# A two-layer recurrent kernel: waits for low halves moved into the last pass of each product, the choice of experts split and moved, its counting matmuls in bf16

## The chip, the cores and the metric

The kernel runs on one core of a Trainium2 chip. The metric is the device time of one execution in microseconds; the median of several executions is compared. The engines are TensorE (PE; its weight loads are shown as PEld), VectorE (DVE), ScalarE (ACT), GpSimd (POOL) and SyncE (SP, which here only issues DMAs).

## What is computed

The input is x of shape (8, 512, 128) in float32. Two layers follow, each of the form x = x + s * silu(f), where s is a sequence mixer and f a feed-forward branch, both of the layer-normed x.

```python
# second layer, attention branch: a memory MLP per head (w0, w1), 8 heads, chunks of 64 tokens
ss = rmsnorm(seq, store_norm_g)
kv = ss @ w_kv                            # keys, values per head
grads = grad(chunk_loss)(mem_ws, keys, lr, values)
momentum = assoc_scan(mom_gate, -grads)   # over the chunks
updates = assoc_scan(1 - decay, momentum)
x = q @ (mem_w0 + updates[0])
vals = silu(x) @ (mem_w1 + updates[1])
out = (rmsnorm(vals) * (mh_gamma + 1) * gate) @ w_combine
# second layer, feed-forward branch: one of 8 experts for each token
aff = x @ centroids.T
eid = argmax(aff, axis=-1)
alpha = sigmoid(sum(x * centroids[eid]))
out = x + alpha * (relu(ln(x)[expert eid] @ w1[eid] + b1[eid]) @ w2[eid] + b2[eid])
```

The first layer (a gated linear recurrence and a binarized MLP) is not touched by the change.

## The kernel before

The attention branch is computed without ever forming the updated memories: the update of a chunk is a sum over earlier tokens, so that each application of an updated memory is a plain product plus a causal sum of scores times gradients. The scores have 4 row tiles of 128 tokens; the coefficients of the two scans (`m.coef`) are multiplied onto them.

**The heads.** `heads` runs 65 steps over 64 pairs (batch, head). In one step three pairs are in work, and each engine's code for it is one function `step(f, s, z)`: `f` is the pair whose first half is done (keys, the gradient, the first application, which ends as `xs`), `s` the pair before it, in its second half (scores of `xs` against `s_sb`, second application, `vals`, the product with `w_combine`), `z` the pair before that, whose head output is normalized and added to `acc`. Each engine has its own queue and goes through `step` in the order in which it is written; between engines there are only semaphores (`p_`, `a_`, `v_`, `g_` for those that PE, ACT, DVE and POOL raise).

**High and low halves.** Products that need more precision than one pass gives are split: the high half is a rounded copy (fp32r), the low half the difference. `product` then makes three passes into one bank, high times high, high times low and low times high. The high halves are cast on ACT (`s_high` L1053, `qa_high` L1066, `xs_high` L1047, `err_high` L1073). The low halves are subtracted on DVE (`xs_low` in `low_rows`, L1266; `err_low`, L1335) and on POOL (`s_low` and `qa_low` in `lacks`, L1455). PE waits for the low half before the first of the three passes:

```python
for j, (u, v) in enumerate(((0, 0), (0, 1), (1, 0))):
    last = pe.matmul(out, left[u], right[v], start=start and j == 0, stop=stop and j == 2)
```

**A step on PE** goes: projections U, EB and QA (`project`), the scores of `s` (`scores`, three passes for row tiles 0 and 1, then plain float32 matmuls, L790), the product of `w1` with `s_sb` into EB, the same with `xs` into VB and the causal sum (`apply`, L798), four transposes of `err` (L939), the product of `w4t` with `err` into U, the scores of `f`, four transposes of `du`, the projection with `w_x`, `apply`, and at the end the rows out (L978) and sums of squares (L982). In five of the eight batches a block of 128 tokens of the experts runs between these.

**Extras of the first steps.** The last batch's preparation is finished within the heads: in step 0 (`n == 0`) `last_weights`, the normalized last rows (two on ACT, two on POOL in `last_rows_normalized`, L1461) and their transposes (`last_turned`, L832); in step 1 `last_products`. The experts are chosen on DVE in `choose` (9 operations, L1170 to L1178), called in step 1 (`k == 0`) after `weigh` of `s`. The tokens of each expert are then counted on PE in `routing`, two float32 matmuls with 256 columns in steps 2 and 3.

**The tail.** In the last steps DVE also adds up finished batches (`last_sum` L1389, `add_rows` L1396), and in the last step (`final(s)`) it makes `xs_low`, the means, the weighing, `acc`, one `add_rows` for batch 6, `attention_before_last_head` (L1404, L1405), the last means (L1261) and `finish`.

## Time and profile before

| | |
|---|---|
| Median of 3 runs | 1088.19 us (1088.04 to 1088.26) |
| The profiled execution, own time | 1087.95 us |
| Its span | 1086.2 us |
| PE busy | 1058.4 us, 97% of the span |
| DVE busy | 688.6 us, 63% |
| ACT busy | 674.7 us, 62% |
| POOL busy | 558.9 us, 51% |
| Share of the chain that ended last: PE, POOL, DVE | 90%, 4%, 2% |

The granted clock of TensorE was 0.997 of full speed over the span. A busy PE says only that matmuls were in flight, since they are pipelined; whether PE waited is seen in the distance between the starts of two matmuls.

### The profile page before, as it was taken

The page shows a single profiled execution, that of the slowest core. Times are in us where ns is not written, and L with a number is a line of the kernel's source. Part 1 is how long each engine was busy: PE and PEld are TensorE (multiplying, and loading weights), DVE is VectorE, ACT ScalarE, POOL GpSimd, SP SyncE. Part 2 cuts the span into 40 slices and gives each one's busy share as a digit, 9 for nine tenths or more (in the row PEclk, how much of TensorE's full clock was granted, in tenths as well). Part 3 has the DMA queues.
Part 4 walks back from the last instruction along what each step waited for, and adds up shares of the span by engine and source line. Part 5 has one row for each costly group of instructions (what it writes and reads, how often), then busy time and mean ns, then how long its engine had stood idle before and what let it go on. Part 6 is the DMA issues. An engine that isn't in the chain of part 4 may idle for free.

```text
span 1086.2 us, 19002 instructions
## 1 busy us (share of the span) xinstructions
PE 1058.4 (97%) x6595; PEld 892.7 (82%) x6595; DVE 688.6 (63%) x1757; ACT 674.7 (62%) x1353; POOL 558.9 (51%) x571
## 2 busy tenths in 40 slices
PE   6899899999999999999999999999999999999996
PEld 5566788888888888888888888888888888888885
DVE  5787777777755565556555555655565555556786
ACT  6777566676665565656555655656565556566774
POOL 5885444588874344434444443444344444444553
PEclk9999999999999999999999999999999999999998
DMA  7210300000220000000000000000000000004220
GB/s 210 75 53 20 117 1 1 3 31 20 67 59 4 16 11 11 8 19 10 11 8 9 20 11 6 11 21 8 9 10 12 18 9 6 6 3 118 71 70 26
DMA packets 41953, 32.53 MB, mean 30 GB/s; under 512 B 4010, under 2 KB 36492, under 8 KB 41724
## 3 DMA queue, kind: packets, MB, share of 16 engines
q1 hardware_dynamic: 38262, 25.83, 8.3%
q0 software_dynamic: 2272, 4.67, 1.4%
q8 instruction: 54, 0.88, 0.3%
q10 hardware_dynamic: 1326, 0.82, 0.3%
q14 instruction: 39, 0.32, 0.1%
HBM read 18.23 MB, written 13.34 MB: 29 GB/s over the span
## 4 chain that ended last, share of the span: by engine, by line
PE 90%; POOL 4%; DVE 2%; issue 1%; ACT 1%; DMA 0%; ACTq 0%; POOLq 0%; DVEq 0%
PE bank L775 40%; PE bank L798 22%; PE bank L790 6%; PE bank L978 5%; PE bank L933 3%; PE bank L970 3%; PE bank L958 3%; PE bank L939 2%; PE bank L982 2%; PE bank L326 1%; POOL xn L248 1%; POOL rr L264 1%; PE bank L378 1%; PE bank L349 1%; POOL r L244 0%
## 5 line engine op out<-in xcount | busy, mean ns | idle before, releaser
L1222 DVE TENSOR_TENSOR p_sb<-bank,coef 128x512 f32<-128x512 f32 (+3 forms) x512 | 218.4, 482 | 5.0 <-PE bank L775 4.9
L1497 POOL TENSOR_TENSOR sq_rest<-sq,sq_high 128x450 f32<-128x450 f32 x63 | 66.1, 1049 | 238.4 <-ACT sq_high L1097 238.4
L798 PE MATMUL bank<-p_sb,err_t 128*128 128x450 f32 x504 | 130.8, 402 | 0.0
L798 PE MATMUL bank<-p_sb,du_t 128*128 128x450 f32 (+3 forms) x512 | 128.9, 395 | 0.1
L798 PEld LDWEIGHTS bank<-p_sb,err_t 128*128 128x128 f32 x504 | 82.5, 190 | 44.1 <-DVE p_sb L1222 23.7
L1501 POOL TENSOR_TENSOR sq_low<-sq_rest,sq_mid 128x450 bf16<-128x450 f32 x63 | 66.4, 1054 | 97.7 <-ACT sq_mid L1111 97.3
L798 PEld LDWEIGHTS bank<-p_sb,du_t 128*128 128x128 f32 x512 | 82.1, 190 | 41.7 <-issue 23.3
L1279 DVE SCALAR_TENSOR_TENSOR acc<-bank,rg,acc 128x128 f32<-128x128 f32 x220 | 61.7, 343 | 65.4 <-POOL rg L1479 65.4
L1344 DVE SCALAR_TENSOR_TENSOR du<-q_sb,bank 128x512 f32<-128x512 f32 x64 | 44.0, 688 | 83.2 <-PE bank L775 83.1
L1472 POOL TENSOR_TENSOR rs<-ms,neg_half 128x4 f32<-128x4 f32 (+1 forms) x65 | 80.7, 1242 | 30.6 <-DVE ms L1253 24.7
L1051 ACT ACTIVATE s_sb<-bank 128x512 f32<-128x512 f32 x64 | 38.3, 598 | 87.7 <-PE bank L775 87.7
L1455 POOL TENSOR_TENSOR s_low<-s_sb,s_high 128x512 fp32r<-128x512 f32 x64 | 82.6, 1291 | 15.9 <-ACT s_high L1053 15.8
L1045 ACT ACTIVATE xs<-bank 128x450 f32<-128x450 f32 x64 | 35.0, 547 | 89.3 <-PE bank L798 89.3
L1093 ACT COPY vals<-bank 128x450 f32<-128x450 f32 x63 | 33.7, 535 | 81.1 <-PE bank L798 81.1
L1354 DVE TENSOR_TENSOR xl_all<-bank,xl_all 128x128 f32<-128x128 f32 x39 | 11.4, 292 | 114.3 <-PE bank L970 114.3
L1511 POOL DMA_INDIRECT ffn_rows<-xl_all,ids x39 | 40.4, 1037 | 81.9 <-DVE xl_all L1354 81.9
L1455 POOL TENSOR_TENSOR qa_low<-qa,qa_high 128x450 fp32r<-128x450 f32 x64 | 74.2, 1159 | 14.1 <-ACT qa_high L1066 12.7
L1071 ACT COPY err<-bank 128x512 f32<-128x512 f32 x64 | 37.6, 587 | 60.2 <-PE bank L775 59.5
L978 PE MATMUL bank<-w_out,vals 128*128 128x128 f32 x504 | 66.2, 274 | 0.0
L1108 ACT COPY du_t<-bank 128x512 f32<-128x512 f32 x64 | 37.6, 587 | 35.6 <-PE bank L958 35.6
L978 PEld LDWEIGHTS bank<-w_out,vals 128*128 128x128 f32 x504 | 59.1, 179 | 0.0
L790 PE MATMUL bank<-qa,yb 128*128 128x66 f32 (+1 forms) x256 | 52.8, 288 | 0.0
(341 smaller groups left out, 3089.7 us busy)
## 6 DMA issues: line engine op xcount, KB each, us to landing
sorted_rows<-coef SPq DMA_DIRECT2D x5, 516.0 KB, 5.2
rows<-sorted_rows SPq DMA_DIRECT2D x39, 64.5 KB, 1.8
ew<-in_L_ffn_w SPq DMA_DIRECT2D x8, 256.0 KB, 4.1
x<-in_L_attn_inputs SPq DMA_DIRECT2D x7, 256.0 KB, 5.6
x_rows<-x SPq DMA_DIRECT2D x7, 256.0 KB, 2.3
attn_out<-acc SPq DMA_DIRECT2D x7, 256.0 KB, 2.1
ew<-attn_out SPq DMA_DIRECT2D x7, 256.0 KB
ew<-ffn_rows SPq DMA_DIRECT2D x8, 192.0 KB
```

Source lines behind the costliest of these rows:

```text
L775: last = pe.matmul(out, left[u], right[v], start=start and j == 0, stop=stop and j == 2)
L790: last = pe.matmul(out, left[:, (i - 2) * P:(i - 1) * P], right[:, P * i:], start=True, stop=True)
L798: last = pe.matmul(out[:, P * i:QW], rows[:, i, :], p_sb[:, P_COL[i]:P_COL[i] + QW - P * i], start=False, stop=True, skip_group_check=True)
L978: pe.matmul(VB[0:r, t * P:t * P + P], vals[:, t * P:t * P + r], m.w_out[:, s[1], :], start=True, stop=True)
L1222: last = nc.vector.tensor_tensor(dst, src, w, ALU.mult)
L1279: last = nc.vector.scalar_tensor_tensor(sums, o, g, sums, ALU.mult, ALU.add)
L1344: nc.vector.scalar_tensor_tensor(du[:], q_sb[:], 0.5, U[:], ALU.mult, ALU.mult).then_inc(v_du, 1)
L1455: nc.gpsimd.tensor_tensor(parts[1][:], whole[:], parts[0][:], ALU.subtract).then_inc(done, 1)
L1472: nc.gpsimd.tensor_tensor(rs[:, part], ms[:, part], m.neg_half[:, 0:T][:, part], ALU.pow).then_inc(g_rs, 1)
L1497: nc.gpsimd.tensor_tensor(sq_rest[:], sq[:], sq_3[0][:], ALU.subtract).then_inc(g_rest, 1)
L1501: nc.gpsimd.tensor_tensor(sq_3[2][:], sq_rest[:], sq_3[1][:], ALU.subtract).then_inc(g_lo, 1)
L1511: nc.gpsimd.indirect_dma_start(m.ffn_rows, bass.IndirectOffsetOnAxis(ids[r][:, 0:1], axis=0), y[r], None).then_inc(s_y[r], 16)
```

## The change

It has these parts.

1. `product` makes its passes in the order high-high, low-high, high-low (left, right), so that the right side's low half is used in the last pass only. With `low=` PE waits for that half just before the last pass, and for the high half before the first. This is used at four places of a step: scores of `s` (`v_xl`), the product with `s_sb` (`g_sl`), with `err` (`v_el`), scores of `f` (`g_ql`).
2. `choose` is cut in two. `ranked` (the four operations that find the best expert) runs in step 1 after `err_low`, and the rest after `weigh` of `f` at the end of DVE's step 1.
3. The one-hot choice and the two constant matrices of the counting matmuls are made in bf16: two casts on DVE in `choose`, and `routing` takes them. They lie in the second half of `oh`'s old space.
4. Two of the last four rows are normalized on DVE in place of POOL, ahead of `q_sb` in step 0. `last_turned` stands on PE ahead of the transposes of `err`.
5. In the last step `add_rows` for batch 6 runs on DVE before `weigh`.

```diff
-            def product(out, left, right, start=True, stop=True):
-                for j, (u, v) in enumerate(((0, 0), (0, 1), (1, 0))):
+            def product(out, left, right, start=True, stop=True, low=None):
+
+                for j, (u, v) in enumerate(((0, 0), (1, 0), (0, 1))):
+                    if j == 2 and low is not None:
+                        pe.wait_ge(*low)
                     last = pe.matmul(out, left[u], right[v], start=start and j == 0, stop=stop and j == 2)
...
-                        last = product(out, [part[:, i * P:i * P + P] for part in left_2], [part[:, P * i:] for part in right_2])
+                        last = product(out, [part[:, i * P:i * P + P] for part in left_2], [part[:, P * i:] for part in right_2], low=low if i == 0 else None)
...
-                    pe.matmul(FREE, m.upper[:], flat, start=True, stop=True).then_inc(p_routed, 1)
+                    pe.matmul(FREE, upper16, flat, start=True, stop=True).then_inc(p_routed, 1)
                 if c == 2:
-                    pe.matmul(FREE, m.ones[:], flat, start=True, stop=True).then_inc(p_routed, 1)
+                    pe.matmul(FREE, ones16, flat, start=True, stop=True).then_inc(p_routed, 1)
...
-                    pe.wait_ge(v_xl, k + 1)
+                    pe.wait_ge(a_xh, k + 1)
                     pe.wait_ge(v_p0, SC_BANKS * (k + 1))
-                    scores(s_2[s[1] % 2], xs_2, s_sb[s[1] % 2][:, 2 * P:], xs, p_s1)
+                    scores(s_2[s[1] % 2], xs_2, s_sb[s[1] % 2][:, 2 * P:], xs, p_s1, low=(v_xl, k + 1))
...
-                    pe.wait_ge(g_sl, n + 1)
+                    pe.wait_ge(a_sh, n + 1)
...
-                    product(EB[:], [w[:] for w in w1], [part[:] for part in s_2[h % 2]], start=False).then_inc(p_e, 1)
+                    product(EB[:], [w[:] for w in w1], [part[:] for part in s_2[h % 2]], start=False, low=(g_sl, n + 1)).then_inc(p_e, 1)
...
                 if f is not None:
+                    if n == 0:
+                        last_turned()
                     pe.wait_ge(a_err, n + 1)
...
-                    if n == 0:
-                        last_turned()
-                    pe.wait_ge(v_el, n + 1)
+                    pe.wait_ge(a_eh, n + 1)
                     pe.wait_ge(v_q, n + 1)
-                    product(U[:], [w[:, 3, :] for w in m.w4t], [part[:] for part in err_2]).then_inc(p_d, 1)
+                    product(U[:], [w[:, 3, :] for w in m.w4t], [part[:] for part in err_2], low=(v_el, n + 1)).then_inc(p_d, 1)
...
-                    pe.wait_ge(g_ql, n + 1)
+                    pe.wait_ge(a_qh, n + 1)
...
-                    scores(yk, qa_2, yw, qa, p_s0, SC_ORDER[:-1])
+                    scores(yk, qa_2, yw, qa, p_s0, SC_ORDER[:-1], low=(g_ql, n + 1))
...
+            def last_rows_normalized():
+                for k in range(2, T):
+                    row = NT - T + k
+                    last = nc.vector.tensor_scalar(m.xl_all[:, row, 0:D], m.x_last[:, k, :], m.mv[:, row, 0:1], m.rr[:, 1, row:row + 1], ALU.subtract, ALU.mult)
+                last.then_inc(v_last, 1)
...
-            def choose():
+            def ranked():
 
                 link(nc.vector.tensor_reduce(top, m.aff, AX.X, ALU.max))
                 link(nc.vector.tensor_tensor(oh, m.aff, bc(top), ALU.is_equal))
                 link(nc.vector.tensor_tensor(oh, oh, m.rank_f[:], ALU.mult))
                 link(nc.vector.tensor_reduce(best, oh, AX.X, ALU.max))
-                nc.vector.tensor_tensor(oh, m.rank_f[:], bc(best), ALU.is_equal).then_inc(v_oh, 1)
+
+            def choose():
+
+                nc.vector.tensor_copy(upper16, m.upper[:])
+                nc.vector.tensor_copy(ones16, m.ones[:])
+                nc.vector.tensor_tensor(oh16, m.rank_f[:], bc(best), ALU.is_equal).then_inc(v_oh, 1)
...
                 if final(s):
                     low_rows(k)
                     means(l)
+                    add_rows(B - 2)
                     dve.wait_ge(p_x, k + 1)
...
-                    if k == 0:
-                        dve.wait_ge(g_last, POOL_LAST["roots"])
-                        dve.wait_ge(a_last, ACT_LAST["products"])
-                        choose()
                 if f is not None:
+                    if n == 0:
+                        last_rows_normalized()
                     dve.wait_ge(a_th, n + 1)
...
+                    if n == 1:
+                        dve.wait_ge(a_last, ACT_LAST["products"])
+                        ranked()
                 for c in summed(z)[1]:
-                    if c < B - 1:
+                    if c < B - 2:
                         add_rows(c)
...
                     weigh(f, p_s0, v_p0, n, s)
+                    if n == 1:
+                        dve.wait_ge(g_last, POOL_LAST["roots"])
+                        choose()
...
-                    if n == 0:
-                        last_rows_normalized()
                     scatter(s, 0)
```

DVE in step 1, before, from the last piece of `weigh` of `s` (`p_sb`) on; the tiles named `ew` are scratch of the choice:

```order
L1222 TENSOR_TENSOR p_sb<-bank,coef 128x256
L1170 TENSOR_REDUCE ew<-amd 128x32
L1171 TENSOR_TENSOR ew<-amd,ew 128x256
L1172 TENSOR_TENSOR ew<-ew,rank_f 128x256
L1173 TENSOR_REDUCE ew<-ew 128x32
L1174 TENSOR_TENSOR ew<-rank_f,ew 128x256
L1175 RECIPROCAL ew<-rr 128x32
L1176 TENSOR_TENSOR rr<-rr,ew 128x32
L1177 TENSOR_TENSOR ew<-ew,rr 128x32
L1178 TENSOR_TENSOR ew<-ew 128x32
L1328 SCALAR_TENSOR_TENSOR q_sb<-bank,s_sb 128x512
```

The same place now, to the end of `choose` (in between, `weigh` of `f` with the taking of the gates, L1256):

```order
L1240 TENSOR_TENSOR p_sb<-bank,coef 128x256
L1345 SCALAR_TENSOR_TENSOR q_sb<-bank,s_sb 128x512
L1347 SCALAR_TENSOR_TENSOR q_sb<-thu,q_sb 128x512
L1352 TENSOR_TENSOR err_low<-err,err_high 128x512
L1183 TENSOR_REDUCE ew<-amd 128x32
L1184 TENSOR_TENSOR ew<-amd,ew 128x256
L1185 TENSOR_TENSOR ew<-ew,rank_f 128x256
L1186 TENSOR_REDUCE ew<-ew 128x32
L1364 SCALAR_TENSOR_TENSOR du<-q_sb,bank 128x512
```

```order
L1240 TENSOR_TENSOR p_sb<-bank,coef 128x256
L1190 CAST ew<-upper 128x128
L1191 CAST ew<-ones 128x128
L1192 TENSOR_TENSOR ew<-rank_f,ew 128x256
L1193 RECIPROCAL ew<-rr 128x32
L1194 TENSOR_TENSOR rr<-rr,ew 128x32
L1195 TENSOR_TENSOR ew<-ew,rr 128x32
L1196 TENSOR_TENSOR ew<-ew 128x32
L1170 TENSOR_SCALAR lr_gate<-lr_gate 128x8x8
```

Nine operations no longer stand between `weigh` and `q_sb`; four stand behind `err_low`, and seven, two of them new, behind the last `p_sb` and ahead of the rates (`lr_gate`) and the gates.

PE in a step without extras, before, from the scores of `s` to the product with `s_sb`:

```order
L775 MATMUL bank<-xs_high,s_high 128x450 [waits v_p0,v_xl]
L775 MATMUL bank<-xs_low,s_high 128x450
L775 MATMUL bank<-xs_high,s_low 128x450
L775 MATMUL bank<-xs_high,s_high 128x322
L775 MATMUL bank<-xs_low,s_high 128x322
L775 MATMUL bank<-xs_high,s_low 128x322
L790 MATMUL bank<-xs,s_sb 128x66
L790 MATMUL bank<-xs,s_sb 128x194
L775 MATMUL bank<-s_high,w1n_high 128x512 [waits g_sl]
L775 MATMUL bank<-s_low,w1n_high 128x512
L775 MATMUL bank<-s_high,w1n_low 128x512
```

And now:

```order
L782 MATMUL bank<-xs_high,s_high 128x450 [waits v_p0,a_xh]
L782 MATMUL bank<-xs_high,s_low 128x450
L782 MATMUL bank<-xs_low,s_high 128x450 [waits v_xl]
L782 MATMUL bank<-xs_high,s_high 128x322
L782 MATMUL bank<-xs_high,s_low 128x322
L782 MATMUL bank<-xs_low,s_high 128x322
L797 MATMUL bank<-xs,s_sb 128x66
L797 MATMUL bank<-xs,s_sb 128x194
L782 MATMUL bank<-s_high,w1n_high 128x512 [waits a_sh]
L782 MATMUL bank<-s_high,w1n_low 128x512
L782 MATMUL bank<-s_low,w1n_high 128x512 [waits g_sl]
```

The number of matmuls is the same; the pass with the right low half (`xs_low`, `s_low`) is the third, and the wait for it stands there.

DVE at the start of step 0, before and now (`xl_all<-x_last` are the two rows):

```order
L1429 SCALAR_TENSOR_TENSOR nm_last<-mv,rr 128x4
L1328 SCALAR_TENSOR_TENSOR q_sb<-bank,s_sb 128x512
L1330 SCALAR_TENSOR_TENSOR q_sb<-thu,q_sb 128x512
L1142 TENSOR_TENSOR w_x_low<-bank,w_x_high 128x512
L1151 TENSOR_SCALAR ew<-ew 128x384 x2
```

```order
L1452 SCALAR_TENSOR_TENSOR nm_last<-mv,rr 128x4
L1154 TENSOR_SCALAR xl_all<-x_last,mv,rr 128x128 x2
L1345 SCALAR_TENSOR_TENSOR q_sb<-bank,s_sb 128x512
L1347 SCALAR_TENSOR_TENSOR q_sb<-thu,q_sb 128x512
L1149 TENSOR_TENSOR w_x_low<-bank,w_x_high 128x512
```

The two rows stand ahead of `q_sb` and so of all that DVE does in step 0.

## Rows read from the trace of the kernel before

**Rows 1.** Groups by form, 300 to 1000 us: count | busy us, mean ns | idle before.

```profile
L775 PE MATMUL bank<-y_high,w_v_high 128*128 128x512 f32 x45 | 17.8, 395 | 0.0
L775 PE MATMUL bank<-y_high,w_v_low 128*128 128x512 f32 x45 | 17.7, 394 | 0.0
```

**Rows 2.** Timeline of step 1: start, us, instruction, idle before and its releaser.

```profile
127.41 0.41 DVE L1170 TENSOR_REDUCE ew<-amd 128x32 f32<-128x256 f32 x1
...
128.50 0.62 ACT L1073 CAST err_high<-err 128x512 fp32r<-128x512 f32 x1
...
129.23 0.42 DVE L1174 TENSOR_TENSOR ew<-rank_f,ew 128x256 f32<-128x256 f32 x1
...
130.26 0.60 PE L939 MATMUL bank<-ident,err 128*128 128x128 f32 x4
...
130.51 0.68 DVE L1328 SCALAR_TENSOR_TENSOR q_sb<-bank,s_sb 128x512 f32<-128x512 f32 x1
...
131.83 0.68 DVE L1335 TENSOR_TENSOR err_low<-err,err_high 128x512 fp32r<-128x512 f32 x1
...
132.57 0.50 PE L775 MATMUL bank<-err_high,w4t_high 128*128 128x512 f32 x1 [1.72 <-DVE err_low L1335]
```

**Rows 3.** Timeline, the end of step 1 and the start of step 2.

```profile
137.21 1.04 POOL L1501 TENSOR_TENSOR sq_low<-sq_rest,sq_mid 128x450 bf16<-128x450 f32 x1 [3.79 <-ACT sq_mid L1111]
137.30 1.85 DVE L1151 TENSOR_SCALAR ew<-ew 128x128 f32<-128x128 f32 x2
...
140.12 0.16 DVE L1252 TENSOR_SCALAR ms<-bank 128x3 f32<-128x3 f32 x1 [0.78 <-DVE ew L1153]
...
141.96 0.37 PE L775 MATMUL bank<-xs_high,s_high 128*128 128x450 f32 x1
```

**Rows 4.** Timeline of step 0.

```profile
110.89 1.28 POOL L1455 TENSOR_TENSOR s_low<-s_sb,s_high 128x512 fp32r<-128x512 f32 x1
...
111.40 0.69 DVE L1328 SCALAR_TENSOR_TENSOR q_sb<-bank,s_sb 128x512 f32<-128x512 f32 x1 [0.40 <-ACT thu L1055]
...
114.96 0.69 DVE L1335 TENSOR_TENSOR err_low<-err,err_high 128x512 fp32r<-128x512 f32 x1 [0.19 <-ACT err_high L1073]
...
115.48 1.18 POOL L1455 TENSOR_TENSOR qa_low<-qa,qa_high 128x450 fp32r<-128x450 f32 x1 [0.86 <-ACT qa_high L1075]
...
116.78 0.69 DVE L1344 SCALAR_TENSOR_TENSOR du<-q_sb,bank 128x512 f32<-128x512 f32 x1 [0.17 <-PE bank L775]
```

**Rows 5.** Timeline, a counting matmul (step 2) and the scores behind it.

```profile
147.93 0.59 PE L812 MATMUL bank<-ew,upper 128*128 128x256 f32 x2
...
148.56 0.37 PE L775 MATMUL bank<-qa_low,y_high 128*128 128x450 f32 x1
```

**Rows 6.** Timeline, scores and the product with s_sb, steps 62 and 63.

```profile
1046.61 0.71 PE L790 MATMUL bank<-xs,s_sb 128*128 128x66 f32 x4
1047.33 0.50 PE L775 MATMUL bank<-s_high,w1n_high 128*128 128x512 f32 x1
...
1060.57 0.71 PE L790 MATMUL bank<-xs,s_sb 128*128 128x66 f32 x4
1061.06 0.50 PE L775 MATMUL bank<-s_high,w1n_high 128*128 128x512 f32 x1
```

**Rows 7.** Timeline of the tail.

```profile
1071.29 0.63 DVE L1266 TENSOR_TENSOR xs_low<-xs,xs_high 128x450 fp32r<-128x450 f32 x1 [1.38 <-ACT xs_high L1047]
...
1071.97 0.47 PE L775 MATMUL bank<-xs_high,s_high 128*128 128x450 f32 x1 [0.71 <-DVE xs_low L1266]
...
1072.97 1.69 DVE L1222 TENSOR_TENSOR p_sb<-bank,coef 128x512 f32<-128x512 f32 x4 [0.92 <-PE bank L775]
...
1075.60 0.68 DVE L1396 TENSOR_TENSOR ew<-ew 128x512 f32<-128x512 f32 x1
...
1076.91 0.69 DVE L1405 TENSOR_TENSOR ew<-ew 128x512 f32<-128x512 f32 x1
...
1077.64 0.59 DVE L1261 TENSOR_SCALAR ms<-bank 128x1 f32<-128x1 f32 x4
```

More of the change, by code:

```diff
@@ L694, in attend @@
         oh = early(NT, E)
+        half = oh.rearrange("p n e -> p (n e)").bitcast(BF16)
+        oh16 = half[:, 0:NT * E].rearrange("p (n e) -> p n e", e=E)
+        upper16, ones16 = half[:, NT * E:NT * E + P], half[:, NT * E + P:NT * E + 2 * P]
         cnt, run = early(E, NT), early(E, NT)
@@ L728, in attend @@
         ACT_LAST = {"w_x": 1, "xl": 2, "w_qk": 3, "y": 4, "products": 5, "sums": 6}
-        DVE_LAST = {"nm": 1, "w_x": 2, "w_qk": 3, "y": 4, "gates": 5}
-        POOL_LAST = {"xl": 1, "roots": 2}
+        DVE_LAST = {"nm": 1, "xl": 2, "w_x": 3, "w_qk": 4, "y": 5, "gates": 6}
+        POOL_LAST = {"roots": 1}
         LAST_W = {"w_x": (m.w_x, m.qt, m.mem0, 5), "w_qk": (m.w_qk, m.qt, m.kt, 6)}
@@ L781, in project, with scores @@
                 return product(out[:, 0:width], [part[:, at[1], :] for part in w], y, stop=stop)
-            def scores(left_2, right_2, left, right, done, tiles=SC_ORDER):
+            def scores(left_2, right_2, left, right, done, tiles=SC_ORDER, low=None):
                 for i in tiles:
@@ L804, in routing @@
                 c = first_head(s)
-                flat = oh.rearrange("p n e -> p (n e)")
+                flat = oh16.rearrange("p n e -> p (n e)")
                 if c == 0:
@@ L829, in last_turned @@
                 pe.wait_ge(a_last, ACT_LAST["xl"])
-                pe.wait_ge(g_last, POOL_LAST["xl"])
+                pe.wait_ge(v_last, DVE_LAST["xl"])
                 for k in range(T):
@@ L1197, in places @@
                 link(nc.vector.tensor_tensor(m.aff, m.aff, run.rearrange("p e n -> p n e"), ALU.add))
-                link(nc.vector.tensor_tensor(m.aff, m.aff, oh, ALU.mult))
+                link(nc.vector.tensor_tensor(m.aff, m.aff, oh16, ALU.mult))
                 link(nc.vector.tensor_reduce(pos, m.aff, AX.X, ALU.add))
@@ L1455, in lacks @@
                 nc.gpsimd.tensor_tensor(parts[1][:], whole[:], parts[0][:], ALU.subtract).then_inc(done, 1)
-            def last_rows_normalized():
-                pool.wait_ge(m.g_r1, B)
-                for k in range(2, T):
-                    n = NT - T + k
-                    last = nc.gpsimd.tensor_scalar(m.xl_all[:, n, 0:D], m.x_last[:, k, :], m.mv[:, n, 0:1], m.rr[:, 1, n:n + 1], ALU.subtract, ALU.mult)
-                last.then_inc(g_last, 1)
             def step(f, s, z):
```

## The prediction

> **What bounds the kernel now.** The table shows TensorE busy for 97% of the span and on 90% of the chain that ended last. A busy PE may still wait, so I went through the starts of its matmuls step by step, taking the same matmul in every step as the yardstick. In the middle of the kernel there is nothing to gain: the steps are alike (13.74 us without experts: L790 from 1046.61 to 1060.57, less a wait of 0.22 in between, [rows 6]), and a matmul with a semaphore wait before it is no longer than one without: `y_high,w_v_high`, which waits for `a_dt`, takes 395 ns, `y_high,w_v_low`, which waits for nothing, 394 [rows 1]. The time that a schedule can change lies at the ends. In step 1 PE stands 1.72 us for `err_low`, because DVE, in order, first worked through the choice of experts [rows 2]. In steps 6, 7, 8, 61 and 62 PE starts a product late because its low half is. In the last step it stands 0.71 us for `xs_low`, and then DVE is the last: the last means wait for DVE, not for PE [rows 7].
>
> **The terms.** The sum is made against the profiled execution (1087.95 us, span 1086.2), 0.24 us under the median of the three runs.
>
> *Step 1, the choice.* DVE begins the choice at 127.41 and reaches `q_sb` at 130.51; `err_low` starts at 131.83 and PE's product at 132.57 [rows 2]. Without the choice there, `q_sb` starts 3.10 us earlier, at 127.41, and `err_low` could at 128.73, but `err_high` is there only at 129.12. So `err_low` runs from 129.15 to 129.85, ahead of the end of PE's transposes (130.86) [rows 2]. The wait is gone altogether. PE's next matmul overlaps a long one before it by 0.22 (1060.57 + 0.71 against 1061.06) [rows 6], so 1.72 + 0.22 = 1.94 us. The four operations of `ranked` (127.41 to 129.23, 1.8 us) now follow `err_low`, on this clock from 129.5 to 131.3; `du` behind them needs the three passes of some 0.4 us that start at 130.6, so not before 131.6: hidden, with 0.3 us to spare.
>
> *The rest of the choice.* It now stands behind the last `p_sb` of step 1: one comparison and four small operations, 1.3 us from L1174's start to `q_sb` [rows 2], and two new casts of 128 columns, at 0.1 to 0.2 each (as the second of L1151's pieces below: 0.13 once free), so 1.6 us if nothing holds it. But POOL's `sq_low` runs there: L1151, at 137.30, two pieces of 128 columns, took 1.85 us. The first can be read off the merged row: `sq_low` ends at 138.25 and only then does a piece of this size get through [rows 3]. A cast or a comparison of two SBUF tensors at this place, between 137.1 and 138.25, waits in the same way, and POOL's next operation (`starts`) may hold the small multiplications once more to about 139.0. So I put the end of `choose` at 139.8 (1.6 if free: 138.7). L1151 then comes when POOL is idle and takes 0.5 in place of 1.85, so DVE reaches the means at about 140.6 in place of 140.12 [rows 3]. ACT waits for `v_top` before it takes `xs`: that sets back `xs_high`, `xs_low` and `s_high` by some 1.1 us against PE's order. `xs_low` would end at 142.6 on this clock, while the third pass of the scores, where it is now waited for, is due at 141.96 + 0.41 = 142.37: PE stands about 0.28. `s_low`, behind `s_high` on POOL, costs as much again. I take a loss of 0.55 us; the bounds are 0 (nothing held) and 1.2 (casts and comparison each held by a POOL operation of its own).
>
> *Counting in bf16.* The two float32 passes of L812 take from 147.93 to where the scores begin to flow. `qa_low` starts at 148.56, normally 0.2 behind `qa_high`, so L812 costs 0.43 us of PE [rows 5]. In bf16 one pass of 256 columns remains: a quarter of the time if the passes go by columns, 0.11, and up to 0.19 if something of the next pass's weight load can't hide under so short a one. Saved 0.24 to 0.32 each, twice: 0.5.
>
> *Low halves in the last pass.* In step 62 the product with `s_sb` starts 0.72 behind L790, in the undisturbed step 63 it starts 0.49 behind: 0.22 us lost to `s_low` [rows 6]. Five such places read 0.12, 0.17, 0.22, 0.29 and 0.21 us by the same yardstick, together 1.0. The third pass starts 0.5 us or more behind the first, longer than any of these waits, so all are gained. In the other 58 steps the low half is there in time and nothing changes; the cover is that PE is late anyway, and without it the price of a late half is now reduced by 0.4 to 0.5.
>
> *Step 0.* Here two terms meet. `last_turned` fills time in which PE waits for `err`, and the product with `err` may start at `err_high`, so its third pass is due at once with `err_low`, some 0.5 us earlier than now; but `du` waits for `w_qk_low` on DVE, so at most 0.26 of it reaches the weighing. Against it stand the two rows on DVE, ahead of `q_sb`. On their own they cost 0.3 each. But POOL's `s_low` runs from 110.89 to 112.17 just then [rows 4]. If they are held as L1151 was [rows 3], `q_sb` starts not at 111.40 but near 112.45. POOL no longer slows the gate terms afterwards, which gives about 0.6 back, and `err_low` would start at 115.2 to 115.45 instead of 114.96. `qa_low` on POOL starts at 115.48 [rows 4], a hair later. If `err_low` is first, step 0 gains about 0.1; if it is behind, it waits until 116.66 and the step loses 0.9. I take 0.1, bounds -0.9 and 0.26.
>
> **A rule of the Trainium skill.** The profile shows a DVE operation released at the end of a POOL operation [rows 3]. The page "SBUF — State Buffer" (section "SBUF: two separate sides") says why: VectorE and GpSimd share one port pair under an exclusive lock, taken by whichever starts first for its whole instruction, and a VectorE operation needs it with two SBUF inputs or in a two-port mode. The trace agrees with it in L1151. It speaks against this change at three places: the rows, the casts, the comparison; with it at its full price the result is the first rival's time, without it the sum would be 0.55 better.
>
> *The tail.* `xs_high` is ready at 1071.26, `xs_low` (0.63 long) ends at 1071.92, and PE starts its first pass at 1071.97 [rows 7]. Now two passes run before that and the third starts at 1071.97: it started 0.52 later before. So PE is 0.52 us earlier from there. On DVE the weighing could start at 1072.45, but `add_rows` (0.60 from start to start) now stands before it, from 1071.98 to 1072.58, so it starts 0.39 earlier than 1072.97. What followed `acc` loses the same `add_rows` of 0.60: L1405, before at 1076.91, and the means at 1077.64 come 0.39 + 0.60 = 0.99 earlier, at 1076.65. PE's sums, which the means also need, were there at about 1077.17 by the starts of their matmuls in the timeline, so now at 1076.65: they just meet. Behind this POOL and DVE go on alone, unchanged. 0.98 us, bounds 0.5 (only PE's share) and 1.0.
>
> **Sum.** 1.94 - 0.55 + 0.5 + 1.0 + 0.1 + 0.98 = 3.97 us. 1087.95 - 3.97 = 1083.98; with the 0.24 to the median, 1084.2.
>
> **The rivals.**
>
> *POOL holds DVE at each place.* `err_low` falls behind `qa_low` in step 0 (-0.9 in place of +0.1) and the choice costs 1.2 in place of 0.55. For it: the 0.03 to 0.3 us of margin at 115.48 [rows 4], and that L1151 was held in full. Against it: `err_low` is still computed to be first, and POOL has less to do. 3.97 - 1.0 - 0.65 = 2.3: 1085.9 us. Chance 0.2.
>
> *The low halves buy nothing.* If what delays PE in the five places and the tail follows it (POOL's chain begins with PE's own results, so an earlier PE could meet the next late half), 1.0 and up to 0.5 are missing: 2.5 us, 1085.7. Against it: each chain has slack of over 0.3 in the next product. Chance 0.1.
>
> *A wait inside a product costs PE.* Four waits stand between passes in each of some 63 steps, 252 in all. A wait before a first pass costs nothing that 395 against 394 ns could show [rows 1], but no row has one inside an accumulation. At 16 ns each the whole gain is gone; from 25 ns the kernel is slower by more than 0.2%; at 35 ns it is 8.8 - 4.0 = 4.8 us slower: 1093 us. The mechanism would be a weight load that can't be brought forward past the wait. Against it: the product's first pass has the same load behind a wait and shows none. Chance 0.05.
>
> *Nothing is held.* The two rows and the choice slip past POOL: 3.97 + 0.55 + 0.15 = 4.7: 1083.5. Chance 0.15.
>
> **Chances and range.** The forecast itself, between 1083.8 and 1085.0, has 0.5. With the free case below and the held one above, 1083.2 to 1086.2 holds 8 in 10. The measurement tells about 0.2% (2.2 us) from no change, so faster means under 1086.0: 0.86; within it 0.1; slower 0.04.
>
> **What would show it.** PE's product with `err` in step 1 starts within 0.4 us of the transposes. The counting matmuls are single bf16 rows, and steps 2 and 3 are 0.25 shorter. The scores in step 2 stand for `xs_low` by 0.3, or not at all. In steps 61 and 62 the distance of 0.72 is 0.49. The last means start 1 us earlier, counted from `xs_low`. In step 0 the start of `err_low` against that of `qa_low` decides 1 us. The prediction is wrong if the passes of the middle steps grow longer, or if a DVE operation ahead of `du` is held beyond 131.6.

## The result and the profile after

The changed kernel takes 1082.07 us in the median of 4 runs (1081.69 to 1082.58), the kernel before 1088.22 (1088.04 to 1089.08, 4 runs). The ratio is 0.9939, with a 95% interval of 0.9927 to 0.9951: 6.1 us faster, where 4.0 were forecast, and below the stated range. Its profiled execution is the slowest of the four, 1082.58 us with a span of 1080.8; against that of before it is 5.37 us faster.

A step of PE is measured here from the first matmul `y_high,w_u_high` of a step to that of the next, in the timelines of both profiled executions. Grouped, they say where the time came from:

| PE's steps | before, us | after, us | gain | forecast |
|---|---|---|---|---|
| ahead of step 0 (first layer) | 108.59 | 108.85 | -0.26 | 0 |
| 0 | 12.86 | 13.00 | -0.14 | 0.1 |
| 1 | 18.44 | 16.51 | 1.93 | 1.94 |
| 2 and 3 | 28.30 | 27.92 | 0.38 | -0.05 |
| 6, 7, 8, 61, 62 | 70.19 | 68.75 | 1.44 | 1.0 |
| 4, 5, 9 to 16, 56 to 60 | 205.87 | 204.94 | 0.93 | 0 |
| 17 to 55 (with experts, mostly) | 613.17 | 612.85 | 0.32 | 0 |
| 63 and the tail | 28.79 | 28.01 | 0.78 | 0.98 |

The part ahead of step 0, which the change does not touch, differs by up to 1.5 us between the executions profiled for this study (107.93 to 109.39); that is more than the spread between the four executions of either kernel (1.0 and 0.9 us). The lengths of the steps without experts from 4 on repeat within 0.03 us where an edit does not touch them. Some steps with experts do not repeat as well: step 50 differs by up to 0.35 us between kernels that are the same there, and it is 0.31 longer in the trace after than in that before.

The DVE timeline of the kernel after, at the places of [rows 2, 3, 4, 7] (start, duration, engine, line, operation; in brackets the idle time before it and its releaser):

```profile
111.17 1.60 DVE L1154 TENSOR_SCALAR xl_all<-x_last,mv,rr 128x128 f32<-128x128 f32 x2
112.69 0.68 DVE L1345 SCALAR_TENSOR_TENSOR q_sb<-bank,s_sb 128x512 f32<-128x512 f32 x1
...
115.82 0.69 DVE L1352 TENSOR_TENSOR err_low<-err,err_high 128x512 fp32r<-128x512 f32 x1
...
127.84 0.68 DVE L1345 SCALAR_TENSOR_TENSOR q_sb<-bank,s_sb 128x512 f32<-128x512 f32 x1
...
129.58 0.69 DVE L1352 TENSOR_TENSOR err_low<-err,err_high 128x512 fp32r<-128x512 f32 x1 [0.33 <-ACT err_high L1080]
...
131.55 0.42 DVE L1186 TENSOR_REDUCE ew<-ew 128x32 f32<-128x256 f32 x1
132.13 0.69 DVE L1364 SCALAR_TENSOR_TENSOR du<-q_sb,bank 128x512 f32<-128x512 f32 x1 [0.16 <-PE bank L782]
...
135.56 0.22 DVE L1190 CAST ew<-upper 128x128 bf16<-128x128 f32 x1
135.69 0.22 DVE L1191 CAST ew<-ones 128x128 bf16<-128x128 f32 x1
135.83 1.26 DVE L1192 TENSOR_TENSOR ew<-rank_f,ew 128x256 bf16<-128x256 f32 x1
137.02 0.34 DVE L1193 RECIPROCAL ew<-rr 128x32 f32<-128x32 f32 x1
...
140.18 0.63 DVE L1284 TENSOR_TENSOR xs_low<-xs,xs_high 128x450 fp32r<-128x450 f32 x1 [0.78 <-ACT xs_high L1054]
...
1066.63 0.63 DVE L1284 TENSOR_TENSOR xs_low<-xs,xs_high 128x450 fp32r<-128x450 f32 x1 [1.39 <-ACT xs_high L1054]
...
1067.91 1.67 DVE L1240 TENSOR_TENSOR p_sb<-bank,coef 128x512 f32<-128x512 f32 x4
...
1072.26 0.22 DVE L1279 TENSOR_SCALAR ms<-bank 128x1 f32<-128x1 f32 x2
1072.95 0.22 DVE L1279 TENSOR_SCALAR ms<-bank 128x1 f32<-128x1 f32 x2 [0.46 <-PE bank L881]
```

The same execution on POOL, at the two places where DVE is held:

```profile
111.15 1.28 POOL L1478 TENSOR_TENSOR s_low<-s_sb,s_high 128x512 fp32r<-128x512 f32 x1
115.73 1.78 POOL L1478 TENSOR_TENSOR qa_low<-qa,qa_high 128x450 fp32r<-128x450 f32 x1 [3.30 <-ACT qa_high L1082]
...
135.69 1.12 POOL L1515 TENSOR_TENSOR sq_low<-sq_rest,sq_mid 128x450 bf16<-128x450 f32 x1 [1.92 <-ACT sq_mid L1118]
```

And PE: step 0's wait, and in step 1 the product of [rows 2], which stood 1.72 us and now follows its transposes at once:

```profile
115.57 0.40 PE L782 MATMUL bank<-err_high,w4t_low 128*128 128x512 f32 x1
116.56 0.50 PE L782 MATMUL bank<-err_low,w4t_high 128*128 128x512 f32 x1 [0.59 <-DVE err_low L1352]
...
130.69 0.60 PE L948 MATMUL bank<-ident,err 128*128 128x128 f32 x4
131.05 0.48 PE L782 MATMUL bank<-err_high,w4t_high 128*128 128x512 f32 x1
```

So the two rows hold `q_sb` in step 0 until 112.69, and the comparison is held by `sq_low` (1.26 us, starting 0.14 behind it), both as computed. The counting matmul is one bf16 row, and the second pass of the scores starts 0.34 behind it, where in [rows 5] it was 0.63:

```profile
146.66 0.28 PE L819 MATMUL bank<-ew 128*128 128x256 bf16 x1
...
147.00 0.37 PE L782 MATMUL bank<-qa_high,y_low 128*128 128x450 f32 x1
```

What was not computed is the middle of the kernel. It is visible in a row that the prediction did not use: the weight loads (PEld) of the product with `s_sb`, grouped by line and form. The last columns are busy time, mean ns and the idle time before them with its releaser; first the kernel before:

```profile
L775 PEld LDWEIGHTS bank<-s_high,w1n_high 128*128 128x128 f32 x64 | 12.1, 189 | 3.8 <-POOL s_low L1455 1.2
```

and after:

```profile
L782 PEld LDWEIGHTS bank<-s_high,w1n_high 128*128 128x128 f32 x64 | 12.2, 190 | 0.9
```

2.9 us of idle time at this one load are gone. Step by step in the trace before, 1.31 of the 3.8 lie in the five steps that I had counted, and another 1.31 in the fifteen other steps without experts, 4, 5, 9 to 16 and 56 to 60; after the change both are 0.

### The profile page after: what moved, and what is told of

Read it like the earlier page. It is cut to its first block, busy times and chain, and to the rows that moved or that the text cites. A ratio compares the mean times of both kernels' runs of the same rounds, so it can differ in the third digit from the quotient of the medians.

```text
span 1080.8 us, 18999 instructions
## 1 busy us (share of the span) xinstructions
PE 1055.8 (98%) x6593; PEld 892.0 (83%) x6593; DVE 689.8 (64%) x1761; ACT 674.6 (62%) x1353; POOL 557.4 (52%) x569
## 4 chain that ended last, share of the span: by engine, by line
PE 92%; POOL 4%; DVE 1%; issue 1%; ACT 1%; DMA 0%; ACTq 0%; POOLq 0%; DVEq 0%
PE bank L782 40%; PE bank L805 22%; PE bank L797 6%; PE bank L985 5%; PE bank L977 3%; PE bank L940 3%; PE bank L965 3%; PE bank L948 3%; PE bank L989 2%; PE bank L326 1%; POOL xn L248 1%; PE bank L349 1%; POOL rr L264 1%; PE bank L378 1%; PE bank L282 1%
```

## The experiments

Twelve kernels ran. The edits are against the changed kernel where the label begins with a or n, against the kernel before where it begins with b. Step lengths are PE's, as above.

### The order of the passes alone (b0_order_only)

```diff
-                for j, (u, v) in enumerate(((0, 0), (0, 1), (1, 0))):
+                for j, (u, v) in enumerate(((0, 0), (1, 0), (0, 1))):
```

> The kernel before with the passes of a product in the new order alone; every wait stays before the first pass. Theory (what was missed is a wait of some 0.06 us for the low half of s_sb in every step without experts): the order alone gives nothing, 1088.2 us, and steps 9 to 16 stay at 13.73 us. Rival (the order of the passes shortens the passes themselves): those steps fall to 13.67 and the time to about 1086.7 us.

Measured: 1087.26 us (11 runs) against 1088.05, ratio 0.9993 (0.9984 to 1.0002). No step but one with experts (27, by 0.16) moved by more than 0.05 us, and the steps 9 to 16 did not become shorter (13.74), which refutes the rival. So the order by itself shows no gain clear of noise. The median is 0.8 us lower all the same, within its interval; the profiled executions differ by 0.1.

### Part 1 alone (b1_low_only)

```diff
+                    if j == 2 and low is not None:
+                        pe.wait_ge(*low)
...
-                    pe.wait_ge(g_sl, n + 1)
+                    pe.wait_ge(a_sh, n + 1)
...
-                    product(EB[:], [w[:] for w in w1], [part[:] for part in s_2[h % 2]], start=False).then_inc(p_e, 1)
+                    product(EB[:], [w[:] for w in w1], [part[:] for part in s_2[h % 2]], start=False, low=(g_sl, n + 1)).then_inc(p_e, 1)
```

(and the same for the three other products, with the new order)

> The kernel before with part 1 alone, new order and waits for the low halves before the third pass. Theory: 1.4 us from 24 steps without experts, 1.0 from the five places, 0.5 in the tail, and in steps 0 and 1 another 0.3 and 0.55 because two passes now run during the waits there: 3.7 us faster, 1084.5 us. Rival (low halves are worth only what was forecast): 2.3 us, 1085.9 us, with steps 9 to 16 at 13.73 us.

Measured: 1083.77 us (5 runs), ratio 0.9956 (0.9942 to 0.9969). 4.3 of the 6.1 us are part 1. By steps: 0.26 in step 0, 0.43 in step 1, 0.12 in steps 2 and 3, 1.42 in the five steps, 0.88 in the fifteen other steps without experts, 0.48 in the tail. Another 0.58 in the steps 17 to 55 is there with the new order alone too (612.59 here, 612.58 in b0), and 0.80 was lost ahead of step 0.

### All waits before the first pass, high and low (a1_wait_first)

```diff
-                    if j == 2 and low is not None:
+                    if j == 0 and low is not None:
```

> The changed kernel with all four waits for low halves back before the first pass. Theory: steps 9 to 16 at 13.72 us again, the five places and the tail lose 1.5, step 2 another 0.5 or more since xs_low and s_low are late there: 3.4 us slower than the changed kernel, about 1085.5 us. Rival (the gain beyond the forecast is elsewhere): 1.5 to 2 us slower, about 1084 us.

Measured: 1088.39 us (11 runs), ratio 1.0001 (0.9992 to 1.001): nothing is left of the gain, where I had expected about half. The steps 9 to 16 take 13.79 us, more than before the change (13.73). Here the first weight load of the product with `s_sb` waits for two semaphores. It starts 114 or 115 ns after `s_low` ends, and the matmul behind it 144 to 146 ns, in each of the twenty steps without experts from 4 to 62. With one wait (before, and in the next two kernels) these are 51 to 53 ns for the load and 53 or 54 ns for the matmul. Step 12 of this kernel (`s_low` ends at about 281.90):

```profile
280.61 1.29 POOL L1478 TENSOR_TENSOR s_low<-s_sb,s_high 128x512 fp32r<-128x512 f32 x1
```

```profile
282.01 0.19 PEld L782 LDWEIGHTS bank<-s_high,w1n_high 128*128 128x128 f32 x1
...
282.04 0.47 PE L782 MATMUL bank<-s_high,w1n_high 128*128 128x512 f32 x1
```

So this run charged the old arrangement with something that it did not have.

### The wait for s_low alone before the first pass (a2_sl_first)

```diff
-                    pe.wait_ge(a_sh, n + 1)
+                    pe.wait_ge(g_sl, n + 1)
...
-                    product(EB[:], [w[:] for w in w1], [part[:] for part in s_2[h % 2]], start=False, low=(g_sl, n + 1)).then_inc(p_e, 1)
+                    product(EB[:], [w[:] for w in w1], [part[:] for part in s_2[h % 2]], start=False).then_inc(p_e, 1)
```

> The changed kernel with only the wait for the low half of s_sb back before the first pass; the other three stay inside. Theory: nearly all of the loss of the former, without the tail: steps 9 to 16 at 13.72 us, steps 6, 8, 61 and 62 lose 0.8 together, step 2 0.5: 2.6 us slower than the changed kernel, about 1084.7 us. Rival (the small wait belongs to xs_low or qa_low, not to s_low): steps 9 to 16 stay at 13.67, about 1083.3 us.

Measured: 1085.48 us (8 runs, 1084.28 to 1086.69), ratio 0.9975 (0.9965 to 0.9986). The fifteen steps take 205.91 us, as before the change (205.87), the five 69.96 (70.19), step 2 14.53 in place of 14.12; steps 0 and 1 and the tail keep their gain. This one wait is the whole difference in the fifteen steps, and 1.21 of the 1.44 us in the five; step 7 keeps most of its gain (0.18 of 0.24), so it waited mostly for another half.

### Only the low waits, before the first pass (a6_low_waits_only)

The edit of a1, and the four waits for high halves (`a_xh`, `a_sh`, `a_eh`, `a_qh`) taken out, which makes one wait for a half of each product again.

> The changed kernel with the four low halves waited for before the first pass and the waits for the high halves taken out, so that each product has one wait as before the change. Theory (in every step without experts s_low ends some 0.05 to 0.08 us after PE could start the product with s_sb, and the change gained exactly that): the steps 9 to 16 take 13.73 us again in place of 13.67, steps 6, 7, 8, 61 and 62 are 0.2 to 0.4 longer, the tail 0.5; in all 3.2 to 3.8 us slower than the changed kernel, span 1084.0 to 1084.6. In the run that had both waits before the first pass those steps took 13.79 and the span was 1085.9: by this theory the other 0.06 a step was the price of the second wait on a late half. Rival (the second wait is free, the wait for a late low half costs all of it): steps 9 to 16 take 13.79 again and the span is 1085.9.

Measured: 1087.8 us (11 runs), ratio 0.9995 (0.9986 to 1.0004). The fifteen steps take 206.16 us: 0.63 less than in a1 (206.79), where the waits for high halves stood beside those for low ones, and 1.22 more than in the changed kernel. Of that 0.97 is the late `s_low`, as a2 shows with this wait alone; the other 0.25 comes with the other three waits, and which of them it is stays open. The steps 9 to 16 take 13.77, between the theory's 13.73 and the rival's 13.79, so the theory holds in its main part: the second wait has a price, and the single one costs most of what was gained. The total missed it, by step 0: 14.44 us in place of 13.00. PE stood 1.42 us for `err_low`, and the matmuls behind that ran at half their pace. The timeline of PE, and the windows of 2 us (busy time of PE, PEld, DVE, ACT, POOL, then the granted clock, DMA share, GB/s):

```profile
116.64 0.76 PE L782 MATMUL bank<-err_high,w4t_high 128*128 128x512 f32 x1 [1.42 <-DVE err_low L1348]
117.20 0.63 PE L782 MATMUL bank<-err_high,w4t_low 128*128 128x512 f32 x1
```

```profile
114.00:116.00 2.00, 0.66 (x5) 0.42 (x4) 1.82 (x6) 1.97 (x4) 0.29 (x1) 1.00 0.85 299
116.00:118.00 2.00, 1.35 (x3) 1.15 (x4) 1.09 (x2) 1.70 (x5) 2.00 (x2) 0.66 0.99 323
118.00:120.00 2.00, 2.00 (x8) 1.81 (x7) 1.60 (x3) 0.00 (x0) 1.45 (x2) 0.50 0.99 272
120.00:122.00 2.00, 2.00 (x14) 1.68 (x14) 1.97 (x5) 0.59 (x1) 0.00 (x0) 0.98 1.18 401
```

(0.50 is 1.2 of 2.4 GHz.) In a1, PE stood 1.38 us at the same place and the clock stayed at 1.00; its step 0 took 13.49. So some 0.95 us are the clock, the rest the wait (one trace of each). The 11 runs of a6 fall into two groups (four at 1085.96 to 1086.35, seven at 1087.58 to 1088.94); only one of them has a trace, and the clock granted over the whole span does not tell the groups apart (0.995 and 0.997 in the faster, 0.995 to 0.998 in the slower), so whether the drop in clock parts them is not shown. Either way parts 2 to 5 without part 1 are worth next to nothing: the 1.93 of step 1 is eaten by `err_low`, which part 4 makes late, and by the choice in step 2 (14.58).

### Counting in float32 (a4_f32_count)

```diff
-                nc.vector.tensor_copy(upper16, m.upper[:])
-                nc.vector.tensor_copy(ones16, m.ones[:])
-                nc.vector.tensor_tensor(oh16, m.rank_f[:], bc(best), ALU.is_equal).then_inc(v_oh, 1)
+                nc.vector.tensor_tensor(oh, m.rank_f[:], bc(best), ALU.is_equal).then_inc(v_oh, 1)
...
-                    pe.matmul(FREE, upper16, flat, start=True, stop=True).then_inc(p_routed, 1)
+                    pe.matmul(FREE, m.upper[:], flat, start=True, stop=True).then_inc(p_routed, 1)
```

> The changed kernel with the one-hot choice, the two constant matrices and the counting in float32 again, without the two casts. Theory: the two counting matmuls cost 0.24 to 0.32 more each, and DVE is spared two casts (0.13 each) ahead of the comparison, which POOL's sq_low holds all the same: steps 2 and 3 together 0.4 to 0.5 longer, span 1081.2 to 1081.3. Rival (the counting hides behind a wait of PE in the same step, for the scores' operands): under 0.15 longer in the two steps together.

Measured: 1082.32 us (5 runs), ratio 0.9953 (0.994 to 0.9967). The median can't be told from the changed kernel's. Step 3 is 0.29 longer, as expected; step 2 is not (14.11). Its three small waits (0.11, 0.08 and 0.11 us in the changed kernel, for `xs_low` and twice at `s_low`'s product) are gone instead, since without the casts the comparison starts 0.13 ahead of `sq_low` and is not held. DVE and POOL in this kernel:

```profile
135.56 0.42 DVE L1190 TENSOR_TENSOR ew<-rank_f,ew 128x256 f32<-128x256 f32 x1
135.90 0.35 DVE L1191 RECIPROCAL ew<-rr 128x32 f32<-128x32 f32 x1
136.28 0.65 DVE L1192 TENSOR_TENSOR rr<-rr,ew 128x32 f32<-128x32 f32 x1
136.96 0.71 DVE L1193 TENSOR_TENSOR ew<-ew,rr 128x32 f32<-128x32 f32 x1
```

```profile
135.69 1.18 POOL L1513 TENSOR_TENSOR sq_low<-sq_rest,sq_mid 128x450 bf16<-128x450 f32 x1 [1.92 <-ACT sq_mid L1118]
136.84 0.78 POOL L1472 TENSOR_TENSOR ew<-lr_gate,starts 128x256 f32<-128x256 f32 x1
```

The two products of 32 columns take 0.65 and 0.71 here where the same take 0.40 and 0.19 after the change: POOL holds them in place of the comparison. What is left is 0.34 us: `top` is ready at 137.90 in place of 138.24. The two casts undo in step 2 what the faster counting gives there.

### The whole choice at its old place (a3_choose_back)

```diff
+                    if k == 0:
+                        dve.wait_ge(g_last, POOL_LAST["roots"])
+                        dve.wait_ge(a_last, ACT_LAST["products"])
+                        ranked()
+                        choose()
```

(and both calls of step 1 taken out)

> The changed kernel with the whole choice of experts (its two new casts too) back at its old place, ahead of q_sb in step 1. Theory: q_sb comes 3.4 us later, but PE's product with err in step 1 now waits in its third pass only; with the pass waits alone step 1 took 18.01, and the two casts add 0.26, so 18.2 to 18.3 against 16.51; step 2 loses its three small waits and takes 13.8 in place of 14.12. Together 1.4 to 1.5 slower than the changed kernel: span 1082.2 to 1082.3. Rival (the whole 1.92 comes back): step 1 takes 18.4 or more.

Measured: 1083.34 us (5 runs), ratio 0.9955 (0.9941 to 0.9968). Step 1 takes 18.28 us, step 2 13.80: 1.77 lost and 0.32 won, as the theory has it. PE's product in step 1 stands 0.75 for `q_sb` and 0.53 for `err_low`; part 1 had already taken off a part of the 1.72.

### The rows back on POOL (a5_rows_pool)

```diff
                     lacks(s_sb[h % 2], s_2[h % 2], g_sl)
+                    if n == 0:
+                        last_rows_normalized()
```

(with `nc.gpsimd` in it, and taken off DVE)

> The changed kernel with the two last rows normalized on POOL again. Theory: DVE reaches q_sb of step 0 at once, not after 1.5 us of rows held by s_low, so err_low and the product with err in step 0 come earlier: step 0 takes 12.6 us, as in the run with the pass waits alone, in place of 13.0, and the kernel is 0.4 faster than the changed one. Rival (POOL's rows delay qa_low, and PE waits for that in place of err_low): step 0 takes 12.9 to 13.0, no difference.

Measured: 1081.67 us (5 runs), ratio 0.9946 (0.9933 to 0.996). Step 0 takes 12.73: 0.27 faster than with part 4, between the theories. Now PE stands 1.44 us for POOL's rows ahead of their transposes. Making the rows on DVE costs 0.27 us, and with the earlier place of the transposes, which this run keeps, part 4 costs 0.41: with part 1 alone (b1), rows on POOL and transposes late, step 0 took 12.59.

### add_rows late again (a7_add_late)

```diff
                     means(l)
-                    add_rows(B - 2)
```

(and `c < B - 1` in the loop)

> The changed kernel with add_rows for batch 6 behind the weighing and acc again, in the last step. Theory: the weighing starts 0.1 earlier but the last means are 0.5 later, when DVE ends add_rows and the two operations behind it: the tail is 0.3 to 0.5 us longer (with the pass waits alone it was 28.31 against 28.01). Rival (PE's sums, not DVE, release the last means since the tail's product starts earlier): under 0.1.

Measured: 1082.95 us (5 runs), ratio 0.9956 (0.9942 to 0.9969). The tail takes 28.31 in place of 28.01. Part 5 is worth 0.30 us, not the 0.5 that my sum had for it.

### Towards a better version (n1, n2, n3)

n1 puts the two rows behind both operations of `q_sb`:

```diff
-                    if n == 0:
-                        last_rows_normalized()
                     dve.wait_ge(a_th, n + 1)
...
                     if n == 0:
+                        last_rows_normalized()
                         last_low("w_x")
```

> The changed kernel with the two rows on DVE behind both q_sb operations of step 0, not ahead of them. Theory: at 111.2 POOL's s_low holds the lock, and q_sb, which reads PSUM and one SBUF tensor, can run meanwhile; at 112.6 POOL is done and the rows take 0.28 each, so err_low starts 0.7 earlier (115.1 on the changed kernel's clock) and ahead of qa_low: step 0 takes 12.4 to 12.6 in place of 13.0, the span is 0.4 to 0.6 shorter. Rival (PE's transposes of the last rows come later and cost it as much): step 0 12.8 to 13.0.

Measured: 1081.53 us (5 runs), ratio 0.9939 (0.9926 to 0.9953). Step 0 takes 12.59 in place of 13.00. That is what it took with part 1 alone (b1), so even at this place part 4 gains nothing; it only stops costing. The rows are free there:

```profile
112.40 0.69 DVE L1345 SCALAR_TENSOR_TENSOR q_sb<-thu,q_sb 128x512 f32<-128x512 f32 x1
113.01 0.60 DVE L1154 TENSOR_SCALAR xl_all<-x_last,mv,rr 128x128 f32<-128x128 f32 x2
```

n2 spreads the rest of the choice: casts, reciprocal and two products behind the clearing of `acc` in step 0 (where DVE was idle for 1.4 us), the first reduction ahead of `err_low`, comparison and last product ahead of `du` in step 1. The constants go to the space of `cnt`, which is free until the counts come.

> The changed kernel with the rest of the choice spread: the casts, the reciprocal and two products at the end of step 0, where DVE stood 1.4 us idle, the first reduction ahead of err_low, the comparison and the last product ahead of du in step 1. Theory: nothing stands behind the last p_sb of step 1, so DVE reaches the means of step 2 at about 137 and step 2 loses its three small waits (0.11, 0.08, 0.11) : 13.8 us in place of 14.12; step 1 is 0 to 0.15 longer if du starts later than now. Span 0.15 to 0.3 shorter. Rival (du is late by the comparison and PE's transposes wait for it): step 1 0.3 longer, no gain.

Measured: 1082.33 us (5 runs), ratio 0.995 (0.9936 to 0.9964). Step 1 is unchanged (16.51), step 2 takes 13.79 in place of 14.12: the 0.3 is there by the steps, though it can't be told in the medians.

n3 has both edits.

> Both of the last two edits. Theory: the gains add, since they lie in different steps: 0.6 to 0.9 us shorter than the changed kernel, span 1079.9 to 1080.2, median 1081.2 to 1081.5. Rival (one of the two gains is lost): span 1080.3 to 1080.8.

Measured: 1081.66 us (5 runs, 1081.14 to 1082.57), ratio 0.9942 (0.9928 to 0.9956). The gains add by steps, 12.59 in step 0 and 13.79 in step 2, and the span of 1079.4 is the shortest of all; 0.67 of its 1.43 us under the changed kernel's lie ahead of step 0 and are no merit of the edit. The other 0.74 us of steps 0 and 2 are 0.07% of the time and lie within the spread of the medians.

## Why the prediction was wrong

**The step that failed** is the sentence on the low halves: "In the other 58 steps the low half is there in time and nothing changes". In all twenty steps without experts from 4 on `s_low` was late, by an amount too small to stand out. Step 12 of the kernel before, with POOL (start and duration, so the end is at about 282.59), the weight load some 50 ns behind it, and what went before:

```profile
281.29 1.30 POOL L1455 TENSOR_TENSOR s_low<-s_sb,s_high 128x512 fp32r<-128x512 f32 x1
```

```profile
282.24 0.30 PEld L790 LDWEIGHTS bank<-xs,s_sb 128*128 128x128 f32 x2
282.64 0.19 PEld L775 LDWEIGHTS bank<-s_high,w1n_high 128*128 128x128 f32 x1
```

The same step after the change, where the load follows the one before it at once:

```profile
279.33 0.30 PEld L797 LDWEIGHTS bank<-xs,s_sb 128*128 128x128 f32 x2
279.61 0.19 PEld L782 LDWEIGHTS bank<-s_high,w1n_high 128*128 128x128 f32 x1
```

Before, 0.10 us lie between the end of one load (282.54) and the start of the next; after, none. Of that 0.06 us reach PE's step, in fifteen steps 0.93 us. I had taken the same matmul in other steps as the yardstick, and "the undisturbed step 63", 0.49 us, carried the same wait:

```profile
1059.71 1.29 POOL L1455 TENSOR_TENSOR s_low<-s_sb,s_high 128x512 fp32r<-128x512 f32 x1 [0.22 <-ACT s_high L1053]
```

```profile
1060.80 0.19 PEld L790 LDWEIGHTS bank<-xs,s_sb 128*128 128x128 f32 x1
1061.06 0.19 PEld L775 LDWEIGHTS bank<-s_high,w1n_high 128*128 128x128 f32 x1
```

A comparison of like with like can't show a loss that all of them have. For the same reason the five places were undersized, each by about 0.09: 1.44 in place of 1.0. In the 39 steps from 17 to 55 the 0.32 us can't be put down to it: the order of passes alone, with the old waits, shows 612.58 there against 612.85 after.

**Term by term**, in the order of the sum:

- *Step 1*, 1.94: measured 1.93. `err_low`, `ranked` and `du` came where they were computed (129.58, 132.13), though `du` had 0.16 us to spare and not 0.3: the prediction let `ranked` begin at 129.5, before the 129.85 at which it has `err_low` end. But it is not additive: part 1 alone takes 0.43 of the same wait (b1), and with part 1 in place the move of the choice is worth 1.77 in this step (a3).
- *The rest of the choice*, -0.55: measured -0.33 (14.12 against 13.79 in n2). The mechanism is as forecast: only the comparison is held by `sq_low`, ACT waits for `v_top`, `xs_low` and `s_low` are late for their third passes. `xs_low` costs PE 0.11 us, `s_low` 0.19. The matmul behind the third pass starts 0.31 and 0.34 after it, and in a4, where nothing is late, 0.20 and 0.23; with `s_low` the third pass itself is 0.08 late too:

```profile
140.86 0.47 PE L782 MATMUL bank<-xs_low,s_high 128*128 128x450 f32 x1
141.17 0.31 PE L782 MATMUL bank<-xs_high,s_high 128*128 128x322 f32 x1
...
142.72 0.50 PE L782 MATMUL bank<-s_low,w1n_high 128*128 128x512 f32 x1
143.06 0.36 PE L782 MATMUL bank<-xs_high,w1n_high 128*128 128x450 f32 x1
```

`choose` itself ended where it was put: at 138.24, which is 139.8 on the prediction's clock, since step 1 began 0.40 later here and was 1.93 shorter. What came behind it was shorter than I put it: `xs_low` ended at 140.81, which is 142.3 there and not 142.6.
- *Counting*, 0.5: 0.30 each (step 3 with and without, 14.09 and 13.80), 0.6 together. That is the upper end of the bounds; nothing of the short pass stuck out from under a weight load.
- *Low halves*: above; 1.44 + 0.93 in place of 1.0, and 0.06 in each of steps 2 and 3 (b1).
- *Step 0*, +0.1: measured -0.14. POOL held the rows as forecast, the whole gain of the pass waits there (0.26, b1) was lost with it. The rows' place costs 0.41 (n1). `err_low` started at 115.82, which is 115.56 on the prediction's clock and later than the 115.2 to 115.45 of the sum. The feared case, `err_low` held behind `qa_low` for 0.9, did not come all the same.
- *The tail*, 0.98: measured 0.78, 0.48 of it the pass waits (b1), 0.30 `add_rows` (a7). PE and DVE were to "just meet" at the last means; in fact the second pair of means waits 0.46 for PE's sums, so that the last 0.2 of DVE's gain has no use.

In sum the forecast terms other than the low halves came out at 1.93 - 0.33 + 0.60 - 0.14 + 0.78 = 2.84, where they were put at 2.97. The error is the low halves, 1.44 + 0.93 + 0.12 = 2.49 against 1.0. With the 0.32 of the steps 17 to 55 and the 0.26 lost ahead of step 0 that is 5.39, the 5.37 between the profiled executions; the other 0.8 us of the 6.1 between the medians are within the spread of single executions, and no trace shows where they lie. The low halves' 1.49 us too little are enough by themselves to leave the range: 1084.2 less 1.49 is 1082.7, under its lower end of 1083.2.

**The rivals.** *POOL holds DVE at each place*: half right, held twice, but at 0.41 and 0.33 us and not 1.0 and 1.2. *The low halves buy nothing* is refuted by b1 and a2. *A wait inside a product costs PE* is refuted: with one wait in the third pass the steps became shorter, not longer, and where the low halves are in time (in all but one of the steps 17 to 55 for `s_low`) the waits cost nothing that can be seen: the steps 17 to 55 take 612.59 us with them (b1) and 612.58 without (b0). What does cost is a second wait on one weight load if its event is late (the matmul starts 145 ns behind it in place of 54). *Nothing is held* came nearest in its number and is wrong in its mechanism.

**The rule** of the page "SBUF — State Buffer" of the Trainium skill (section "SBUF: two separate sides"), that VectorE with two SBUF inputs and a GpSimd operation that reads SBUF lock each other out for a whole instruction and that the first one wins, is borne out by the comparison: 0.42 us when it starts 0.13 ahead of `sq_low`, 1.26 when 0.14 behind. By the recorded starts it is not borne out in step 0 of the changed kernel: `qa_low` starts 0.09 ahead of `err_low`, yet it is `qa_low` that takes 1.78 (1.29 in n1, where `err_low` is 0.43 ahead) and `err_low` its usual 0.69. That a start in the trace is not the moment at which the lock is taken would explain it; no run here shows it.

## What to carry to other kernels

A yardstick taken from steps of the same kernel only shows what differs between them. A wait that is in every step must be looked for by itself: take the end of the producer and the start of the consumer's weight load, and see whether the one follows the other at a fixed distance (here 51 to 53 ns in all twenty steps without experts from 4 to 62); if it does, the consumer waits, however regular it looks. Where one operand of a product in passes is late, let the pass that needs it stand last and wait there alone, and give a weight load one wait and not two. And when an experiment puts a wait back, put back the old number of waits too: a1 had one more than before, and overstated what it was to measure.

## What the runs showed of the hardware

- Release of PE by a semaphore of POOL: with one wait on the weight load it starts 51 to 53 ns after the end of the producer and its matmul 53 or 54 ns; with two waits (a1) 114 or 115 and 144 to 146 ns (20 steps each).
- DVE operations of 32 columns with two SBUF inputs, 0.19 us when free, took 0.65 and 0.71 beside POOL operations of 1.18 and 0.78. The casts of 128 columns, with one SBUF input, took 0.22 there as they do elsewhere (0.22 to 0.23); but one started 0.13 ahead of `sq_low` and the other with it, so this does not show whether a cast behind a POOL operation is held.
- After a wait of PE of 1.42 us, ahead of which it had been partly idle, the granted clock was 0.66 and then 0.50 (1.2 of 2.4 GHz) in the windows from 116 to 120 us; 1.38 us at the same place in another kernel left it at 1.00.
